# State products of a Mamba block as three products of rounded high and low parts

## The reference, cut to what matters

```python
xch = (hs * dt[..., None]).reshape(b, nc, CHUNK, H, P)
A_cum = jnp.cumsum(A_dt, axis=-1)
decay_states = jnp.exp(A_cum[..., -1:] - A_cum)
states = jnp.einsum('bzlhn,bhzl,bzlhp->bzhpn', Bc, decay_states, xch)
new_states = jnp.einsum('bhzc,bchpn->bzhpn', decay_chunk, states_p)
Y_off = jnp.einsum('bzlhn,bzhpn,bhzl->bzlhp', Cc, prev, jnp.exp(A_cum))
```

## Time and profile before

| | before |
|---|---|
| median of 3 runs | 1816.5 us (1815.61 to 1817.68) |
| the profiled execution, its own time | 1816.65 us |
| its span, first to last instruction | 1814.8 us |
| TensorE, matmul | 1747.2 us, 96%, 9688 records |
| DVE | 1287.6 us, 71%, 2154 |
| ACT | 1025.9 us, 57%, 1732 |
| POOL | 945.6 us, 52%, 732 |
| mean granted TensorE clock | 0.992 |

### The profile page before, as it was taken

The page is one execution under the profiler, slowest core; times in us unless marked ns, Lnnn a source line. Parts: engine busy times, 40 slices in busy tenths (PEclk is TensorE's granted clock), DMA queues, the critical chain, the costliest instruction groups (busy, mean ns, idle before and its releaser), DMA issues.

```text
span 1814.8 us, 31204 instructions
## 1 busy us (share of the span) xinstructions
PE 1747.2 (96%) x9688; PEld 1332.9 (73%) x9688; DVE 1287.6 (71%) x2154; ACT 1025.9 (57%) x1732; POOL 945.6 (52%) x732
## 2 busy tenths in 40 slices
PE   6889999999999999999999999999999999999978
PEld 4667778777777777777777777777777777877756
DVE  4766677767766678766777677667787667876776
ACT  6556555665546556465555655465564555566544
POOL 1445464555545565354645555455653546566651
PEclk9899999999999999999999999999999999999999
DMA  6312121111212122121211212121211212212111
GB/s 228 104 36 73 56 71 46 43 62 52 76 29 73 50 66 56 27 73 56 67 52 36 67 51 79 29 73 45 70 55 30 71 56 70 66 51 65 62 47 58
DMA packets 80789, 112.44 MB, mean 62 GB/s; under 512 B 28385, under 2 KB 32481, under 8 KB 79842
## 3 DMA queue, kind: packets, MB, share of 16 engines
q1 hardware_dynamic: 62754, 77.71, 14.6%
q10 hardware_dynamic: 17856, 32.51, 5.4%
HBM read 87.90 MB, written 22.29 MB: 61 GB/s over the span
## 4 chain that ended last, share of the span: by engine, by line
issue 48%; POOL 35%; PE 9%; ACT 3%; DVE 2%; DMA 1%; SPq 1%; POOLq 1%; ACTq 0%; DVEq 0%
POOL yt L1737 10%; POOL ssq L1732 7%; POOL prev L1716 5%; POOL wg_lo L1642 4%; POOL wo_lo L1642 3%; POOL yt L1740 3%; POOL wx_lo L1642 2%; PE bank L492 2%; PE bank L494 2%; PE bank L493 2%; PE bank L667 1%; PE bank L745 1%; PE bank L873 1%; DMA gate<-w_mod_dram 0%; POOL rstd L1698 0%
## 5 line engine op out<-in xcount | busy, mean ns | idle before, releaser
L1737 POOL TENSOR_TENSOR yt<-yt,ea 128x384 f32<-128x384 f32 (+1 forms) x128 | 189.5, 1480 | 384.9 <-DVE ea L1550 384.9
L1520 DVE TENSOR_TENSOR lm<-lm,cbm 128x512 f32<-128x512 f32 x256 | 189.4, 780 | 161.8 <-ACT lm L1135 161.8
L1331 DVE SCALAR_TENSOR_TENSOR xc<-bank,bpar,xc 128x511 f32<-128x511 f32 (+2 forms) x384 | 285.2, 743 | 6.8
L492 PE MATMUL bank<-h_hi,wg_hi 128*128 128x512 f32 x640 | 262.4, 410 | 20.7 <-ACT gate L1081 11.3
L494 PE MATMUL bank<-h_hi,wg_lo 128*128 128x512 f32 x640 | 251.6, 393 | 0.0
L493 PE MATMUL bank<-h_lo,wg_hi 128*128 128x512 f32 x640 | 250.6, 391 | 0.0
L492 PE MATMUL bank<-h_hi,wx_hi 128*128 128x512 f32 x512 | 211.5, 413 | 2.2 <-DVE bt L1331 2.2
L492 PE MATMUL bank<-wo_hi,g_hi 128*128 128x512 f32 x496 | 206.6, 417 | 0.0
L494 PE MATMUL bank<-h_hi,wx_lo 128*128 128x512 f32 x512 | 201.3, 393 | 0.0
L493 PE MATMUL bank<-h_lo,wx_hi 128*128 128x512 f32 x512 | 200.9, 392 | 0.0
L494 PE MATMUL bank<-wo_hi,g_lo 128*128 128x512 f32 x496 | 194.8, 393 | 0.0
(11 more groups left out here) (212 smaller groups left out, 3714.2 us busy)
## 6 DMA issues: line engine op xcount, KB each, us to landing
raw_w<-w_in_dram SPq DMA_DIRECT2D x145, 256.0 KB, 2.7
raw_w<-w_out_dram SPq DMA_DIRECT2D x64, 256.0 KB, 2.6
part_d<-part ACTq DMA_DIRECT2D x64, 256.0 KB, 2.2
part<-part_d ACTq DMA_DIRECT2D x60, 256.0 KB, 2.7
rt<-rows_d SPq DMA_DIRECT2D x256, 6.0 KB
acc<-x_dram SPq DMA_DIRECT2D x8, 256.0 KB, 6.7
acc<-w_mod_dram SPq DMA_DIRECT2D x2, 1024.0 KB, 6.1
lh<-neg_d SPq DMA_DIRECT2D x128, 6.0 KB
```

The costliest lines, as they stand in the source:

```text
L492: nc.tensor.matmul(out_ap, whi(k), hhi(k), start=(k == 0), stop=False)
L1331: stt(dst[:, at], ps[:, 0:HALF - 3 + k], w(k), dst[:, at], ALU.mult, ALU.add)\
L1520: tt(lm[:, h % 4, :], lm[:, h % 4, :], cbm[:, toks(hf)], ALU.mult).then_inc(v_m, 1)
L1737: tt(yt[:, j % 2, cols], yt[:, j % 2, cols], ea[:, j % 2, cols], ALU.add).then_inc(p_t3, 1)
```

## The change

`xw`, `bt`, `craw` and `rows` keep their names as views of memory that `xw_lo`, `bt_hi`, `bt_lo` and `xw_hi` take over (the `with ...: pass` frees an address that the next tensor then gets). Outside the last group:

- DVE copies the transposed B out of its banks to `bt_hi` (rounded) and subtracts `bt_hi` from the banks to `bt_lo`, two operations more per group.
- After DVE has written `xw`, ACT copies it to `xw_hi`, POOL subtracts, in place, to `xw_lo`, and TensorE waits for that (x_lo) instead of v_xw.
- The state product becomes `split_product` of depth 1: three fp32r matmuls. 98 products are changed, the 14 of the last group are not.
- On ACT the copies stand behind `silu_gate(1)` (z = 0), behind the first fill of step 1 (z = 1), behind `silu_gate(2)` and its part DMA (z = 2), and behind `silu_gate(3)` (z = 3). On POOL each subtraction is the first thing in its step, and the fills are moved: none ahead of the decay in step 0, one in the others, the rest behind it.

Since `rows` now shares memory with `xw_hi`, unit 0 puts the gate rows into `part`, stores one partition of them to DRAM (`grow_d`, 4 KB), and the last group loads them back with a broadcast to all partitions (512 KB) after all state products of the groups before.

```diff
+        with nc.sbuf_tensor("xw", [128, 2, BLOCK], F) as xw:
+            pass
+        xw_lo = sb("xw_lo", [128, 2, BLOCK], R)
...
                     if last and c == 0:
+                        sp.wait_ge(d_grow, 16)
+                        sp.wait_ge(t_st, states_before(NBLK - 2, 0))
+                        sp.dma_start(flat(rows, 0, 2), grow_d.rearrange("o n -> (o n)").partition_broadcast(128))\
+                            .then_inc(d_rows, 16)
                         sp.wait_ge(a_bcsilu, 2 * GROUPS)
                         x_tile(0)
...
-                    te.wait_ge(v_xw, sb0 + z + 1)
+                    if last:
+                        te.wait_ge(v_xw, sb0 + z + 1)
+                    else:
+                        te.wait_ge(x_lo, sb0 + z + 1)
...
-                    nc.tensor.matmul(bank[7][:, :], bt[:, toks(hf, z, 1)], xw[:, z % 2, :],
-                                     start=True, stop=True).then_inc(t_st, 1)
+                    if last:
+                        nc.tensor.matmul(bank[7][:, :], bt[:, toks(hf, z, 1)], xw[:, z % 2, :],
+                                         start=True, stop=True).then_inc(t_st, 1)
+                    else:
+                        split_product(bank[7][:, :], lambda k: bt_hi[:, toks(hf, z, 1)],
+                                      lambda k: bt_lo[:, toks(hf, z, 1)], lambda k: xw_hi[:, z % 2, :],
+                                      lambda k: xw_lo[:, z % 2, :], 1).then_inc(t_st, 1)
...
+                def split_xw(z):
+                    if not last and z < NZ - hf:
+                        se.wait_ge(v_xw, sb0 + z + 1)
+                        act(xw_hi[:, z % 2, :], xw[:, z % 2, :], ACT.Copy).then_inc(a_xh, 1)
+
                 for z in range(1, NZ):
                     silu_gate(u, c, z)
+                    if z == 1:
+                        split_xw(0)
                     if first and z == 2:
                         for v in range(2):
                             se.wait_ge(t_row, v + 1)
-                            act((ga_row, gb_row)[v], bank[4 + v][:, :], ACT.Copy).then_inc(a_rows, 1)
+                            act(part[:, v, :], bank[4 + v][:, :], ACT.Copy).then_inc(a_rows, 1)
+                        se.wait_ge(a_rows, 2)
+                        se.dma_start(grow_d[:, :], flat(part, 0, 2)[0:1, :])\
+                            .then_inc(d_grow, 16)
...
-                    if z < 3:
-                        for f in (todo[0] if z == 1 else []) + todo[z]:
+                    if z == 1:
+                        for f in todo[0] + todo[1][0:1]:
                             unit_fill(f, g)
+                        split_xw(1)
+                        for f in todo[1][1:]:
+                            unit_fill(f, g)
+                    elif z == 2:
+                        split_xw(2)
+                        for f in todo[2]:
+                            unit_fill(f, g)
+                    else:
+                        split_xw(3)
...
+                            vec.tensor_copy(bt_hi[:, toks(h2)], bank[6 + h2][:, :]).then_inc(v_bh, 1)
+                    if not last:
+                        for h2 in range(2):
+                            ve.wait_ge(v_bh, 2 * g + h2 + 1)
+                            tt(bt_lo[:, toks(h2)], bank[6 + h2][:, :], bt_hi[:, toks(h2)].bitcast(F), ALU.subtract)\
+                                .then_inc(v_bl, 1)
...
                 for z in range(NZ):
 
+                    if not last and z < NZ - hf:
+                        po.wait_ge(a_xh, sb0 + z + 1)
+                        tt(xw_lo[:, z % 2, :], xw[:, z % 2, :], xw_hi[:, z % 2, :].bitcast(F), ALU.subtract).then_inc(x_lo, 1)
                     if z == 0 and not first and c in (0, 3):
                         group_rstd(g - 1 if c == 0 else g, 1 if c == 0 else 0)
-                    for f in todo[z]:
-                        unit_fill(f, g)
+                    if z >= 1:
+                        for f in todo[z][0:1]:
+                            unit_fill(f, g)
                     if z >= 1 - hf and z < NZ - hf:
...
+                    for f in todo[z][1 if z else 0:]:
+                        unit_fill(f, g)
```

More of the change, by code:

```diff
@@ L47, in adaln_mamba_ffn @@
         xdt = sb("xdt", [128, NZ, BLOCK])
-        xw = sb("xw", [128, 2, BLOCK])
+        with nc.sbuf_tensor("xw", [128, 2, BLOCK], F) as xw:
+            pass
+        xw_lo = sb("xw_lo", [128, 2, BLOCK], R)
+        with nc.sbuf_tensor("rows", [128, 2, HID], F) as rows:
+            pass
+        xw_hi = sb("xw_hi", [128, 2, BLOCK], R)
         prev = sb("prev", [128, NZ + 1, BLOCK])
@@ L56, in adaln_mamba_ffn @@
         acc = sb("acc", [128, NT, HID])
-        bt = sb("bt", [128, TOK])
-        craw = sb("craw", [128, TOK])
+        with nc.sbuf_tensor("bt", [128, TOK], F) as bt:
+            pass
+        bt_hi = sb("bt_hi", [128, TOK], R)
+        with nc.sbuf_tensor("craw", [128, TOK], F) as craw:
+            pass
+        bt_lo = sb("bt_lo", [128, TOK], R)
         ct = sb("ct", [128, TOK])
@@ L82, in adaln_mamba_ffn @@
         nmr = sb("nmr", [128, NT])
-        rows = sb("rows", [128, 2, HID])
         bank = [ctx.enter_context(nc.psum_tensor(f"bank{i}", [128, 512], F)) for i in range(8)]
@@ L96, in adaln_mamba_ffn @@
         part_d = scratch("part_d", (NT, 128, HID))
+        grow_d = scratch("grow_d", (1, 2 * HID))
         d_x = [sem(f"d_x{i}") for i in range(NT)]
@@ L119, in adaln_mamba_ffn @@
         a_bias, p_bias = sem("a_bias"), sem("p_bias")
+        a_xh, x_lo, v_bh, d_grow, d_rows = sem("a_xh"), sem("x_lo"), sem("v_bh"), sem("d_grow"), sem("d_rows")
         t_ffn, v_y, v_done, d_out = sem("t_ffn"), sem("v_y"), sem("v_done"), sem("d_out")
@@ L1429, in accumulate @@
                     ge(ve, d_pout[s], 16 * (4 * g1 + 2 * h1 + z // 2))
+                    if isinstance(u, int) and u == 1 and z < 2:
+                        ve.wait_ge(d_grow, 16)
                     vec.tensor_copy(part[:, s, :], bank[4 + s][:, :]).then_inc(v_acc, 1)
@@ L1435, in accumulate @@
                 if end:
+                    ve.wait_ge(d_rows, 16)
                     link(tt(part[:, s, :], part[:, s, :], ga_row, ALU.mult))
@@ L1484, in unit @@
                         ve.wait_ge(t_btr, 2 * g + h2 + 1)
-                        vec.tensor_copy(bt[:, toks(h2)], bank[6 + h2][:, :]).then_inc(v_bl, 1)
+                        if last:
+                            vec.tensor_copy(bt[:, toks(h2)], bank[6 + h2][:, :]).then_inc(v_bl, 1)
+                        else:
+                            vec.tensor_copy(bt_hi[:, toks(h2)], bank[6 + h2][:, :]).then_inc(v_bh, 1)
[4 more added lines that the diff above has]
+                                .then_inc(v_bl, 1)
                 for z in range(NZ):
@@ L1655, in residual @@
                 if t == 0:
-                    po.wait_ge(a_rows, 2)
+                    po.wait_ge(d_rows, 16)
                 po.wait_ge(v_acc, 4 * (UNITS - UPG - 1) + 4 * (t // NZ))
```

1 line of the change is left out of this document (added).

## The result

The changed kernel takes 1818.28 us, the median of 18 runs (1815.94 to 1820.32), against 1815.56 us for the kernel before in 18 runs (1812.98 to 1817.68). The ratio is 1.0015, with an interval of 1.0008 to 1.0021: some 2.7 us slower, which is less than 0.2%, and outside the range of 1804 to 1816 us. Every ratio here is taken over undisturbed runs alone and is not the plain quotient of the two medians beside it; the two differ by up to 0.001.

The account below looks back on a forecast made before the run. The prediction took TensorE's list of work to bound the kernel. Saving 15.2 us, less 0.6 and 3.8 for unit 0 and 5.0 for c = 3, left 5.8 us: 1810.7 us, with an 8-in-10 range of 1804 to 1816 us.

Parts of the forecast that it names:

- What bounds the kernel: Almost the whole span: TensorE's list sets the end, so a cheaper product is worth its price unless other engines take over.
- The product: State products on TensorE: 0.85 us becomes 0.70, saving 0.155 us each, 15.2 us over 98 products.
- ACT, POOL and DVE in c = 0 to 2, the B subtractions, the gate row: Added work in c = 0 to 2, two DVE subtractions per group, gate row reload: hidden, costed at nothing.
- Unit 0: First unit, nothing hides the longer chain: costs 3.8 us (chain 3.4, clock 0.4) and 0.6 us of saving.
- The clock's 0.4 us: Unit 0: a 2.9 us TensorE gap lowers the clock, costing between 0 and 1.7 us; 0.4 taken.
- c = 3: Unit c = 3, seven times: loses its 0.46 us saving and ends 0.25 us later, 5.0 us in all.
- The second rival: In c = 3 two sums are hit, fourth fill 1.4 us late, unit 1.0 later: 1816 us; chance 0.18.
- the fourth fill and SP's list: In c = 3 POOL's late fourth fill delays SP's parameter DMAs and the next weight load: 0.3 or 0.9 us late.
- Rival 1: c = 3 is hidden after all and only unit 0 costs: 10.8 us gained, 1805.7 us; chance 0.22.
- Rival 3: POOL's three splits ahead of the fourth fill make c = 3 end 2.3 us later: 1825.0 us; chance 0.09.
- Rival 4: Each new product pays 0.32 us for its first matmul, so saves only 0.06 us: 1819 us; chance 0.03.
- the same: Outcome within about 0.2% (3.6 us) of no change, between 1812.9 and 1820.1 us; chance 0.26.

Follow-up runs that it names:

- experiment 7: No run of its own: a table comparing the kernels' c = 3 units by fill, copy, product and exponential times; no measured time.
- experiment 10: Changed kernel, in c = 3 ACT copies the fourth weight load behind the table load and POOL lowers it behind its last decay: 1814.95 us, 0.9993.
- experiment 8: Changed kernel, in c = 3 decay behind first sum, second fill ahead of split of z = 1: 1808.75 us; first group also in old form: 1804.34 us.
- experiment 6: Two variants of the changed kernel: POOL's list in its old order, 1814.4 us (0.9996); POOL's 98 subtractions left out, 1800.44 us (0.9912).
- experiment 5: Changed kernel, POOL's decay of z = 0 in c = 3 (not the last group's) waits for DVE's first sum: 1812.88 us, 0.9988.

## Why the prediction was wrong

**What bounds the kernel: right.** No wait at the state product in c = 0 to 2, and what a product saves arrives whole.

**The product: under-sized.** I took 0.85 less 0.70, 0.155 us. The medians over groups 0 to 6 are 0.857 us from the old product to the transposes behind it and 0.685 from the new one: 0.172. In units c = 0 to 2, 73 products gave 13.15 us, 0.18 each against 11.3 us forecast.

**ACT, POOL and DVE in c = 0 to 2, the B subtractions, the gate row: right at nothing.** The units stand at -0.71, -0.55 and -0.71 us, for 4, 3 and 4 products. The first three units of the last group, where the row is loaded back, stand at +0.09 us.

**Unit 0: the chain right, the clock wrong.** The gap of 2.9 us (2.95) and the 3.4 us of the chain (3.37) hold. The clock's 0.4 us was a term of its own, chosen low between 0 and 1.7, and it was 4.2. I looked at the one gap and at the 3.4 us of work that had followed the gap before it. Left out was the second gap ahead of the fourth product (1.54 us), and that matmuls at 1.2 GHz lie on the same chain as the waits. Why the clock falls twice in some executions and once in others, no run shows. This step costs 3.8 us of the 7.9 by which the sum missed.

**c = 3: the step that failed most.** The forecast had +0.25 us, it was +1.11: 6.0 us over seven units. Four things were wrong in it. First, I counted the hit on the first sum only, and let the splits fall into POOL's gaps; the split of z = 1 stands between the first two fills, and hits the second sum as well. The second rival had this ("two of the sums are hit"), at a chance of 0.18, and 1.0 us later against 1.11 measured. Its 1816 us lacks unit 0's clock. Second, it is not the fourth fill and SP's list that carry the delay to the end of the unit, but the second fill, the load behind it, and the table load on ACT (experiment 7; the other route was measured 0.8 us long in experiment 10, when this one was out of the way). Third, "what POOL loses ahead of 891 is lost for the group, save 0.41 us" followed one route, and did not look for another that had 0.6 us to spare and a larger delay. Fourth, the wait of the state product itself was priced in unit 0 and rightly put at nothing in c = 0 to 2, but in c = 3 it had no term at all. It is 0.82 us in each of the seven, always at z = 2, and more than the 0.46 us that the unit's products save.

The rule of the Trainium skill ("SBUF — State Buffer", Who interferes with whom), that DVE with two SBUF inputs and a GpSimd instruction that reads SBUF exclude each other, agrees with the trace: the first two sums meet a POOL operation in all seven c = 3 (1.49 us, and 1.74 to 1.84); the third does not (0.75 us). That a sum so lengthened is itself the cost did not hold: with POOL's new order alone both sums were long, and the kernel was no slower.

**Rival 1** (c = 3 hidden, 0.46 us shorter than before) is not reached even with the mends of experiment 8, where c = 3 is as long as before; without the splits (experiment 6) it is 0.66 us shorter. **Rival 3** had the place right (the splits in POOL's list) and the size too large (2.3 us for 1.1). **Rival 4** is excluded by the records 0.23 us apart. (Its 1819 us also took the cost of c = 3 from the larger saving; with 0.06 us a product it comes to about 1817.6.)

**The chances.** The two misses, 3.8 and 6.0 us, have one sign, and the surplus of 1.8 us on the products did not cover them: -5.8 + 3.8 + 6.0 - 1.8 = +2.2, against +2.06 in the traces. I had let unit 0 move by one microsecond either way, though its clock alone had bounds of 0 and 1.7, and the 4.2 us measured lie outside even these. That the kernel came out within 0.2% of the kernel before is thus no credit to the 0.26 given to "the same": the case in it that came nearest had c = 3 right and unit 0 not.

## What to carry to other kernels

When an engine gets an operation more per step, look for which of its results sets a *buffer* free, not only for who waits for its next result: here a load three microseconds long, and behind it a table load, stood between POOL's second fill and the next stage. An operation ahead of such a release can cost nearly in full, and the same one behind it cost only what its own reader waited, 0.45 us here. In experiments 5 and 8 one wait and one exchange in POOL's list took the seven c = 3 from 7.77 us over before to 0.18. And where a stage runs once, without other work to hide a longer chain, leave the old form in it.

## What the runs showed of the hardware

- Around the same gap of 2.95 us on TensorE the granted clock fell to 0.50, the 1.2 GHz level, in four executions and stayed at 1.00 in two; in these it fell at 113 us, 1.3 and 1.7 us after a gap of 1.54 us. With both gaps filled by useless products the clock stayed at 1.00, and the unit was 4.2 us shorter for doing more.
- At a place that no edit touched, 94 to 98 us, the clock was 1.00 in seven of fourteen traces and 0.50 to 0.61 in seven, and unit 0 then began 1.2 to 2.5 us later.
- The exclusion between VectorE and GpSimd works in both directions: the sum at 888.62 us takes 1.74 us for 0.75, and POOL's subtraction at 889.77 takes 1.74 for 1.30.
- A long sum costs only when something waits for it: with POOL's order changed alone, the two first sums of c = 3 took 1.49 and 1.56 us for 0.75 each, and these units were 0.2 us shorter.
